# Attention on 64 samples: three products of ones in each step, and a new order of the groups around them

## What is computed

```python
h = concatenate([image_rows, text_rows], axis=1)        # 64 x 205 x 64
x = layernorm(h)
q, k, v = (heads(x @ W.T + b) for each of q, k, v)       # 4 heads of 16
attn = softmax(einsum('bhnd,bhmd->bhnm', q, k) * SCALE)
out = einsum('bhnm,bhmd->bhnd', attn, v)
h = h + (bf16(out) @ Wo.T + bo)
h = h + experts(layernorm(h))
```

## Time and profile before

| | us |
|---|---|
| runs: median (lowest, highest) of 3 | 2515.5 (2495.8, 2520.8) |
| the profiled execution, its own time | 2517.8 |
| its span | 2516.0 |
| TensorE busy with products (PE) | 2279.1, 91% |
| TensorE busy with weight loads (PEld) | 1889.1, 75% |
| VectorE (DVE) | 1736.5, 69% |
| ScalarE (ACT) | 1437.5, 57% |
| GpSimd (POOL) | 1144.1, 45% |
| mean granted clock of TensorE | 0.835 |

### The profile page before, as it was taken

The page is one execution under the profiler, slowest core; times in us unless marked ns, Lnnn a source line. Parts: engine busy times, 40 slices in busy tenths (PEclk is TensorE's granted clock), DMA queues, the critical chain, the costliest instruction groups (busy, mean ns, idle before and its releaser), DMA issues. The chain is left out here.

```text
span 2516.0 us, 58817 instructions
## 1 busy us (share of the span) xinstructions
PE 2279.1 (91%) x20145; PEld 1889.1 (75%) x20145; DVE 1736.5 (69%) x5336; ACT 1437.5 (57%) x3034; POOL 1144.1 (45%) x1519
## 2 busy tenths in 40 slices
PE   6999999848999999999999709999999996999998
PEld 6999999747888888888888606777777774666665
DVE  5655555356888888888888655555555554788888
ACT  2222222106888888888888644444444444666663
POOL 4433333105777777777777562222222222434432
PEclk8999999857999999999999855555555555999999
DMA  2000031000000000000000000000000000000000
GB/s 85 15 18 13 13 67 25 1 0 2 2 2 2 2 2 2 2 2 2 2 2 2 2 0 1 1 1 1 1 1 1 1 1 1 8 10 9 8 10 11
DMA packets 38894, 21.13 MB, mean 8 GB/s; under 512 B 28696, under 2 KB 38040, under 8 KB 38554
## 3 DMA queue, kind: packets, MB, share of 16 engines
q1 hardware_dynamic: 38654, 17.97, 2.9%
HBM read 14.60 MB, written 3.36 MB: 7 GB/s over the span
## 5 line engine op out<-in xcount | busy, mean ns | idle before, releaser
L441 PE MATMUL im_c<-im_a_hi,im_w 128*128 128x256 f32 (+2 forms) x1920 | 428.8, 318 | 13.8 <-POOL im_a_lo L351 13.8
L441 PEld LDWEIGHTS im_c<-im_a_hi,im_w 128*128 128x128 f32 x1920 | 322.1, 191 | 30.9 <-POOL im_a_lo L351 14.0
L441 PE MATMUL im_c<-im_a_lo,im_w 128*128 128x256 f32 (+2 forms) x960 | 303.8, 316 | 0.0
L1043 POOL TENSOR_TENSOR tx_KB<-tx_KF,tx_head_rows 128x1248 fp32r<-128x1248 f32 x128 | 289.6, 2263 | 23.3 <-PE tx_scores_t L1328 15.2
L1842 POOL TENSOR_TENSOR at_xs<-at_z,at_xs 128x128 fp32r<-128x128 f32 x64 | 29.0, 453 | 421.9 <-ACT at_xs L1859 421.9
L904 DVE TENSOR_REDUCE tx_mpad<-tx_scores 77x8 fp32r<-77x616 f32 x256 | 202.1, 789 | 2.9 <-PE tx_maxT L1316 1.9
L345 POOL TENSOR_TENSOR im_rstd<-im_var_eps,im_power 128x4 f32<-128x4 f32 x64 | 68.6, 1072 | 284.1 <-DVE im_var_eps L280 284.1
L441 PEld LDWEIGHTS im_c<-im_a_lo,im_w 128*128 128x128 f32 x960 | 183.1, 191 | 8.4
L1174 ACT ACTIVATE tx_PT<-tx_scores_t 77x624 f32<-77x624 f32 x256 | 175.8, 687 | 17.1 <-PE tx_scores_t L1328 4.6
L1328 PE MATMUL tx_scores_t<-tx_QP,tx_KB 128*77 128x78 f32 x2048 | 183.9, 240 | 0.0
L274 DVE BATCH_NORM_STATS2 im_stats<-im_h 128x6 f32<-128x128 f32 (+1 forms) x192 | 47.6, 303 | 192.0 <-ACT im_h L386 111.9
(11 more groups left out here) (316 smaller groups left out, 6472.0 us busy)
## 6 DMA issues: line engine op xcount, KB each, us to landing
im_x<-x SPq DMA_DIRECT2D x16, 384.0 KB, 3.3
out<-h SPq DMA_DIRECT2D x32, 64.0 KB
tx_toks<-x_txt SPq DMA_DIRECT2D x1, 1925.0 KB
im_raw<-L_tok_conv_w SPq DMA_DIRECT2D x1, 1280.0 KB, 8.6
out<-h SPq DMA_DIRECT2D x32, 38.5 KB
im_raw<-L_tok_conv_w SPq DMA_DIRECT2D x1, 960.0 KB, 4.6
im_raw<-L_tok_conv_w SPq DMA_DIRECT2D x1, 640.0 KB, 5.9
tx_raw_W<-L_txt_W SPq DMA_DIRECT2D x2, 256.0 KB, 6.8
```

The source lines that it names most:

```text
L441: last = pe.matmul(acc[:, :, d0:d1], w[c][:, slot, part], img[:, b0_:b1_, d0 + shift:d1 + shift, kj:kj + J], start=opens, stop=closes)
L1043: pool.tensor_tensor(KB[:, q % 2, t], KF[:, t].bitcast(F32).unsqueeze(1).broadcast_to([P, HPT, QW]), head_rows[:].unsqueeze(2).broadcast_t ...
```

## The change

A tile of 128 x 512 ones in bf16 is set once at the start. In each step of attention TensorE multiplies ones by ones three times, 512 columns each, with a stationary operand of 128 x 128. Two of these products go into the first bank of `scores_t`, between the wait for the exponential that frees it and the wait for `q_set`; `score_t` overwrites them right behind. One goes into `of_q`, before `project_q` overwrites it. No result of theirs is read.

The order changes too. On TensorE, `project_o(n - 2)` moves behind `weigh(n)`, and `score(n + 2, 0)` moves up from behind `turn_x` to right behind `score_t(n + 1, 0)`. On VectorE, the copy of the values moves from the end of the step before (`set_v(n + 1)`) to behind the first maximum (`set_v(n)`), and `add_y` behind the second maximum.

```diff
+class Warm:
+    def __init__(self, p):
+        self.rows = p.sb("warm_rows", [P, 512], BF16)
+    def run(self, pe, bank, times):
+        for _ in range(times):
+            pe.matmul(bank, self.rows[:, 0:P], self.rows[:], start=True, stop=True)
...
             for t in clear:
                 pool.memset(t[:], 0.0)
+            pool.memset(warm.rows[:], 1.0)
...
                 def step(n):                      (VectorE)
                     find_max(n + 1, 0)
-                    add_y(n - 2)
+                    set_v(n)
                     row_stats(n + 4)
                     find_max(n + 1, 1)
+                    add_y(n - 2)
                     cut_k(n + 2)
                     join_max(n + 1)
                     mean_and_var(n + 4)
                     cut_q(n + 2)
                     normalise_o(n)
-                    set_v(n + 1)
...
                 def score_t(m, tile):
                     if live(m):
                         at, n = TILES[tile]
-                        if tile == 0:
-                            pe.wait_ge(q_set, m + 1)
                         if m * 2 + tile:
                             pe.wait_ge(exped, m * 2 + tile)
+                        if tile == 0:
+                            warm.run(pe, scores_t[:, 0], 2)
+                            pe.wait_ge(q_set, m + 1)
...
+                def keep_warm(m):
+                    if live(m):
+                        if m >= 1:
+                            pe.wait_ge(q_cut, m)
+                        warm.run(pe, of_q[:], 1)
+
                 def step(n):                      (TensorE)
                     project_k(n + 2)
-                    project_o(n - 2)
+                    keep_warm(n + 2)
                     score(n + 1, 1)
                     weigh(n)
+                    project_o(n - 2)
                     project_q(n + 2)
                     turn_max(n + 1)
                     turn_outs(n)
                     turn_o(n - 1)
                     score_t(n + 1, 0)
+                    score(n + 2, 0)
                     project_v(n + 1)
                     turn_x(n + 3)
-                    score(n + 2, 0)
                     score_t(n + 1, 1)
```

More of the change, by code:

```diff
@@ L496, in _, with constants @@
                 each_quad(pe, step)
-def constants(p, ident, clear):
+def constants(p, ident, warm, clear):
     nc = p.nc
@@ L1576, in norm_rows, with fusion_attention @@
     last.then_inc(normed, 1)
-def fusion_attention(p, inputs, ident, rows_of, both_tiles):
+def fusion_attention(p, inputs, ident, warm, rows_of, both_tiles):
     nc = p.nc
@@ L2449, in early_fusion_embed @@
         expert = ExpertInputs(p, of("L0_ffn_", EXPERT_WEIGHTS))
-        constants(p, ident, [text.cols_all, attention.b_raw, expert.b_raw])
+        warm = Warm(p)
+        constants(p, ident, warm, [text.cols_all, attention.b_raw, expert.b_raw])
         p.begin_stage()
@@ L2456, in early_fusion_embed @@
         p.end_stage()
-        fusion_attention(p, attention, ident, rows_of, lambda n: h[:, n])
+        fusion_attention(p, attention, ident, warm, rows_of, lambda n: h[:, n])
         experts(p, expert, ident, rows_of, out)
```

## The result

The changed kernel takes 2368.7 us (median of 4, 2365.5 to 2372.3) against 2510.6 for before (median of 4, 2495.8 to 2520.8), a ratio of 0.944 with a 95% interval of 0.939 to 0.949. It is faster by some 142 us and lies inside the range of 2275 to 2400, but 53 us above the forecast of 2316 and 21 above 2348, the upper bound of the forecast's own terms. Its profiled execution has a span of 2364.2 us.

What follows compares the result with a forecast made beforehand. Attention was taken to be bound by TensorE at the half clock. From 2517.8 us, 64 steps shortened from 9.23 to 6.0 us take 207, steps before the rise add 5 and a memset 0.3: 2316 us, range 2275 to 2400.

Steps and rivals of the forecast that it cites:

- the forecast's own terms: Bounds from attention's step length: 5.5 us a step gives 2284 us, 6.5 gives 2348; chance 0.74.
- What bounds the kernel: Attention, 597 us: TensorE 99% busy at half clock, 9.23 us a step; every other engine has about half its time free.
- Part one: Three added products on TensorE in attention: 1.29 us a step at the half clock, 0.70 at the full one.
- Part two: TensorE's clock in attention: the products make it rise within the first two full steps, and it stays up.
- Part three: Attention's step at the full clock: TensorE's own work 5.78 us, a loop through ScalarE 5.79, both binding together.
- The loop through the exponentials: Attention's chain score_t(0), exp, score_t(1), exp, weigh, next score_t(0): 5.79 us a step, binding together with TensorE's own work.
- Part four: Moved groups in attention, chiefly score(n + 2, 0) ahead of project_v and turn_x: 0.2 us a step, ends 0 and 0.5.
- A: Rival: attention's clock doesn't rise and the products add 0.97 to 1.29 us a step, 2580 to 2601 us; chance 0.08.
- B: Rival: attention's clock rises and falls repeatedly; 2449 us with half the steps at each level; chance 0.08.
- C: Rival: VectorE's maxima, join and cuts bind attention at 6.5 to 7 us a step; 2380 us at 7.0; chance 0.08.
- The sum: Attention's 64 steps go from 9.23 to 6.0 us: 2517.8 - 207 + 5 + 0.3 = 2316 us.

## Why the prediction came out as it did

**What bounds the kernel**: right. With the clock up and the order of before, the stage is still TensorE's, 99% busy. The share of weight loads, tried beside the busy share, does not tell the levels apart: 75% in attention at 0.50, but 266.3 of 366 us, 73%, with the products at 1.00.

**Part one, the price of a product**: right at the full clock. Three products less one went from 5.91 to 5.70 us, 0.21 each against the 0.235 taken, and the row of another type served. At the half clock one product made the step 9.74 instead of 9.23, 0.51 against 0.43, with the waits of that step not taken apart.

**Part two, the clock**: right that the products lift it and, for the changed kernel, that it rises within the first two steps; the later rises at 1580 to 1622 in other kernels show that the moment was not to be known from the rows used. Wrong in "and the clock to stay": it fell twice, for 6.8 us each. It held without a break where TensorE no longer waited for `project_k`'s x: in the order of before, with only the score put back, and in the new order with `turn_x` early and three buffers. In the three kernels with that wait and products throughout it fell, twice here, five times with only the score up, once in the middle of the stage with `turn_x` early alone. The rise was forecast from the end of the trace, where this mix of work had lifted the clock. That before is itself close to a rise agrees with its two runs of 2467.6 and 2481.8 us.

**Part three, the step at the full clock**: right in size. Own work was put at 5.78 us and the products-only kernel has 5.91. The loop through the exponentials, put at 5.79 with `project_o` moved into it, did not bind: in the kernel with only the score back, which keeps that move, TensorE starts `score_t(1)` and `weigh` with no idle time shown before them.

**Part four, the moved groups, is the term that failed.** It was taken at 0.2 us a step with ends 0 and 0.5, and measured 0.73. Its part on `cut_q` was put at 0 to 0.2 and came at 0.22, but taking that wait away left the step at 6.61. What it did not see lies off TensorE's own queue, in the bank `x_and_k` and the buffers of x. The text named `project_v` and `turn_x` as the groups that are held back, weighed only `score_t(1)` behind them, and did not ask who waits for their results: ScalarE's `set_xT` waits for both, and `project_k` of the next step for it. That was to be read in the kernel before (`act.wait_ge(v_made, m - 1)`, and `take` on the bank). In the order of before the score stood between `turn_x` and `project_k` and covered the two copies.

**Rivals.** A did not happen, but three of the four runs of one product are A, at 2551. B happened in small. C's time (step 6.5 to 7) was where the result fell, though not by its mechanism: it was not VectorE's maxima or cuts but ScalarE's copy. That the range held the result is luck to that extent: it reached up to 2400 for C, and the forecast's own bounds ended at 2348. The chance of 0.08 for C was too small beside a forecast that held a change of order priced from its queue alone.

**The sum**, with 6.64 for 6.0: 0.64 x 64 = 41 us of the 50 by which the profiled execution (2366.0) exceeds 2316, the falls and 6 us behind the stage the rest.

## What to carry to other kernels

A stage whose engine is 99% busy can still be half as fast as it might be: read the granted clock beside the busy share, and if it stays at the lower level try filler products where the engine waits, enough of them and throughout, then count them down; here two of 512 columns in a step of 5.7 us were enough, one was not (but for 37 us in one run), and the values made no difference. Time several runs of each: with the same three products and nothing else changed they differed by up to 30 us. Time filler and reordering apart: here the filler was worth 187 us and the new order gave 38 of them back. For a group that is moved, follow each result of every group that it pushes back, through other engines and buffers, to whoever waits for it.

## What the hardware showed that was not expected

- TensorE 99% busy by the profile for 575 us went with a clock of 0.50 all along, and two more products a step with 1.00 for 320 us.
- Identical runs of one kernel can differ by 218 us where the work is on the edge (2332 to 2550, three products of 256 columns).
- A clock that is up need not stay up by itself: in the new order it fell 21 us after the last product, 34 after the rise, for the rest of the stage.
- The clock may rise without the products: two of 25 runs of the kernel before had a mean clock of 0.859 and 0.852, where the other runs beside the experiments had 0.834 to 0.842.
- A tile of zeros does as well as a tile of ones (2317 to 2347 us against 2318 to 2344).
